# Broadcast copies loaded one chunk at a time over all 128 partitions, and the first tile's work rearranged

## The chip, the cores and the metric

The kernel runs on one core of a Trainium2 chip. The metric is the device time of one execution in microseconds. Engines are named as in the profile: PE (TensorE, with its weight loads PEld), DVE (VectorE), ACT (ScalarE), POOL (GpSimd), SP (SyncE, which here only issues DMAs). An engine name with a q (SPq) is that engine's sequencer issuing DMAs.

## The reference, cut to what matters

```
e  = stack of 32 gathered rows, one per table      # (B=1024, M=32, D=16)
x1 = relu(einsum('bmd,bhd,mhk->bkd', e, e,  W0))   # h over 32
x2 = relu(einsum('bmd,bhd,mhk->bkd', e, x1, W1))   # h over 64, K = 64
x3 = relu(einsum('bmd,bhd,mhk->bkd', e, x2, W2))
z  = concat(sum_d x1, sum_d x2, sum_d x3)          # (B, 192)
h  = concat(z, dense_ctx); two relu layers (512, 256), then one output
```

All of it is in float32.

## The kernel before, in words

The batch is cut into 8 tiles of 128 rows, and each tile into two blocks by the embedding dimension d (8 of 16 values each), so there are 16 blocks of N = 8 x 128 = 1024 columns. A block has three layers. For each layer an engine multiplies pairs of (m, h) rows elementwise into a product tile z of 128 partitions x 2 x 1024, and PE contracts it with a 128x64 weight chunk into the accumulators. Layer 0 has two such pairs and a small extra one; layers 1 and 2 have eight each (four in the order NAT, four in SWP, in which the halves of h are swapped between partitions).

The first factor of a layer-1 or layer-2 product is x1 or x2, which ACT spreads from the accumulators into the banks xq (for DVE) and xs (for POOL). The second factor is `x0b[s]` (s is the half of d): for every chunk c of 8, partition p holds row 4c + p // 32 of the transposed embeddings, so each row of 4 KB is repeated over 32 partitions. A chunk over all partitions is 512 KB, and `x0b[s]` has 8 chunks, 4 MB. Pair j uses chunks 2j and 2j + 1. SP loads it from the DRAM scratch tensor `x0t`, for every block anew, in eight DMAs of 512 KB (`load_x0b`, line 371): one for each group r of 32 partitions and each half of the chunks. The half signals `x0b_in[s][half]`. The two buffers alternate: the one of the next block is loaded while the present block computes, and the load is issued when DVE has finished layer 2 of the block before. `load_l0` (lines 376 to 382) loads what layer 0 of a coming block needs: `x0_rep` (512 KB), four `x0_rot` chunks (512 KB each), `x0_lo` and `x0_hi` (64 KB each). SP issues in program order; in each tile it also writes the next tile's transposed embeddings to `x0t` (line 389, `write_half`) and waits until they are written before the next `load_l0`.

POOL gathers the embedding rows by indirect DMA, 32 for each tile (line 447), spread over the blocks by `gathers(b)`, and makes 3 of the 16 products of a block (line 472); DVE makes the others (line 529, and lines 549 in halves for the first of each layer-2 order).

Tile 0 is different. 13 of its tables are gathered; the other 19 (1000 or 1250 rows) are loaded whole into 125 partitions (line 426), and PE picks the line by a one-hot product (`pick_lines`), DVE masks and sums the row (`mask_rows`, `pick_rows`, lines 642 and 652) into `emb0`. PE transposes the four groups of 128 columns in the order GROUPS = (2, 0, 1, 3) (`transpose_group`), ACT moves them to `emb_t` and issues the writes to `x0t` (`move_first_tile`). Meanwhile the first layer 0 doesn't wait for DRAM: DVE makes its products with batch rows on partitions (line 698, eight of 128x512, `z0`), reading `emb0` with the columns of one table 16 apart; PE transposes them (line 1044), ACT copies them to `z_dve` (line 800). DVE makes the masks (lines 677 to 683) and the symmetric weights of layer 0 (lines 685 to 690) between the picks and these products. SP issues the tables' loads, then all 16 loads of the layer-1 and layer-2 weights `w_cin` (line 430), then `x0b[0]` in 16 DMAs of 256 KB (two chunks at a time, a group as soon as it is written). ACT's queue loads the MLP weights before it does anything else, and ACT orders them (lines 929 and 931) ahead of the first x1.

Of the kernel before, what the change touches and what calls it, by code (L numbers as in the profile page):

```python
# [28 lines left out]
WARM_FIRST_X = 5  # L29
# [6 lines left out]
def cin_tower(nc, dense_t, ids, tables, w0, w1, w2, wt1, bt1, wt2, bt2, wt3, out):  # L36
# [46 lines left out]
    def l1_dve(b):  # L83
        return [(v, j) for v in l1_phases(b) for j in range(PAIRS) if not (v == NAT and j in pool_l1(b))]
# [4 lines left out]
    def l1_order(b):  # L89

        if b == 0:
            return [(NAT, 0), (NAT, 1), (NAT, 2), (NAT, 3), (SWP, 0), (SWP, 1), (SWP, 2), (SWP, 3)]
# [66 lines left out]
    with ExitStack() as ctx:  # L159
# [76 lines left out]
        emb0_wrap = emb0_flat[:, M * D:M * D + M // 2 * D]  # L236
# [4 lines left out]
        def emb0_columns(table, d, dims):  # L241

            whole = x0b[1][:, :, :]
            return bass.AP(whole.tensor, table * D + d, [list(whole.ap[0])] + dims)
# [20 lines left out]
        emb0_wrapped = sem("emb0_wrapped")  # L265
# [10 lines left out]
        mlp_ordered = sem("mlp_ordered")  # L276
        x0b_in = [[sem(f"x0b_in_{s}_{half}") for half in range(2)] for s in range(HALVES)]
# [21 lines left out]
        ze_used = sem("ze_used")  # L299
        x1_ready = [sem("x1_nat_ready"), sem("x1_swp_ready")]  # L300
# [22 lines left out]
        def x0b_ready(t, s, j):  # L323

            first = 2 * 4 * 16 if s == 0 else 4 * 16
            return x0b_in[s][j // 2], 4 * 16 * t + first
# [34 lines left out]

        block = ctx.enter_context(nc.Block())

        @block.sync
        def _(sp):
# [26 lines left out]

            def load_dense(t):
# [3 lines left out]
            def body(t):  # L397
                first_tile, last_tile = isinstance(t, int) and t == 0, isinstance(t, int) and t == TILES - 1
                for k in range(2):
                    if not is_last(t, k):  # L400
# [5 lines left out]
                        for half in range(2):  # L406
                            load_x0b(t + k, 1 - k, CH // 2 * half, CH // 2 * (half + 1))
# [19 lines left out]
            for l, (w, w_in) in enumerate(((w1, w1_in), (w2, w2_in))):  # L427
                for v in (NAT, SWP):
                    for r in range(4):
                        sp.dma_start(w_cin[l][Q * r:Q * r + Q, v, :, :],  # L430
                                     bass.AP(w.tensor, r * K * K + (r + v) % 2 * Q * K,
# [514 lines left out]
        def _(pe):  # L946
# [231 lines left out]
            for i in range(len(BATCHES) + 2):  # L1178
# [4 lines left out]
                if i == 6:  # L1183
                    transpose_group(0)
# [40 lines left out]
```

## Time and profile before

| | us |
|---|---|
| three runs | 630.64, 631.96, 633.41 (median 631.96) |
| the profiled execution | 630.55 |
| its span in the profile | 628.7 |
| granted TensorE clock, mean | 0.984 of full |
| busy: PE, DVE, POOL, ACT | 594.6, 585.8, 443.2, 355.5 |
| DMA | 119.82 MB, mean 191 GB/s |

The span runs from the first to the last instruction of the core; the time of the execution is 1.85 us longer. In the profile a share of the DMA is the mean busy share of the core's 16 DMA engines; where two packets overlap on one, it passes 1. In a stretch cut into 40 slices, a digit is that share in tenths (9 is 0.9 or more).

### The profile page before, as it was taken

Reading aid. Unit: us, or ns where it says so; the run is one execution under the profiler, and the core shown is the slowest. Engines: PE = TensorE matmul, PEld = TensorE weight load, DVE = VectorE, ACT = ScalarE, POOL = GpSimd, SP = SyncE. Lnnn points to the kernel's source line nnn. Section 1 sums busy time; section 2 is a strip of 40 time slices with the busy share of each in tenths; the row PEclk is TensorE's granted clock in tenths of the full one; section 3 lists DMA queues with packets and bytes.
Section 4 is the critical chain, followed back from the end, with each engine's and each line's share of the span. In section 5 each row is a group of like instructions: output and inputs, shape, how many; then the busy total and the mean of one; then the engine's idle time right before and its main releaser. Section 6 shows DMA issues by size and latency. Waiting matters only on the chain.

```text
span 628.7 us, 8924 instructions
## 1 busy us (share of the span) xinstructions
PE 594.6 (95%) x3046; PEld 243.0 (39%) x3046; DVE 585.8 (93%) x398; ACT 355.5 (57%) x665; POOL 443.2 (70%) x305
## 2 busy tenths in 40 slices
PE   4398998999999999999999999999999999999988
PEld 4252332234343354334443354334443354334434
DVE  4759999999999989999999999999999999999873
ACT  0173754729394663829385574829385674829361
POOL 5767887888888884988878887988878460806120
PEclk9579999999999999999999999999999999999999
DMA  6899989994997689695999779795999789690000
GB/s 176 192 236 271 210 249 210 274 211 113 252 264 183 137 248 214 205 218 128 238 218 246 154 231 213 230 217 129 221 216 258 155 247 217 212 213 17 2 0 1
DMA packets 60175, 119.82 MB, mean 191 GB/s; under 512 B 15271, under 2 KB 33734, under 8 KB 60054
## 3 DMA queue, kind: packets, MB, share of 16 engines
q1 hardware_dynamic: 49414, 114.69, 73.7%
q0 software_dynamic: 7584, 1.96, 3.8%
q10 hardware_dynamic: 3152, 2.86, 1.7%
q8 instruction: 13, 0.21, 0.2%
q14 instruction: 12, 0.10, 0.1%
HBM read 115.27 MB, written 5.25 MB: 192 GB/s over the span
## 4 chain that ended last, share of the span: by engine, by line
PE 53%; POOL 21%; DVE 12%; issue 7%; ACT 3%; SPq 2%; DMA 1%; DVEq 0%; ACTq 0%; POOLq 0%
PE acc L968 47%; POOL emb L447 12%; POOL z_pool L472 8%; DVE z_dve L529 8%; PE psm L1071 2%; SPq L426 2%; PE psm L1079 2%; DMA x_rot<-in_tbl_dram 1%; DVE z_dve L549 1%; DVE x0b L698 1%; PE acc L983 1%; ACT xq L717 1%; ACT xq L725 1%; ACT xq L771 1%; PE psm L1086 1%
## 5 line engine op out<-in xcount | busy, mean ns | idle before, releaser
L529 DVE TENSOR_TENSOR z_dve<-xq,x0b 128x2048 f32<-128x2048 f32 x179 | 398.5, 2279 | 12.4 <-ACT xq L717 7.5
L968 PE MATMUL acc<-z_dve,w_cin 128*64 128x512 f32 x1688 | 387.2, 597 | 9.9 <-DVE z_dve L529 7.1
L472 POOL TENSOR_TENSOR z_pool<-x0b,xs 128x2048 f32<-128x2048 f32 x45 | 205.3, 4565 | 89.4 <-ACT xs L717 88.9
L447 POOL DMA_INDIRECT emb<-in_tbl_dram,ids_all x224 | 218.3, 974 | 66.3 <-issue 61.3
L968 PEld LDWEIGHTS acc<-z_dve,w_cin 128*64 128x64 f32 x1688 | 127.3, 136 | 230.5 <-issue 166.9
L754 ACT ACTIVATE xq<-acc 64x512 f32<-64x512 f32 x64 | 36.5, 570 | 123.1 <-PE acc L968 122.4
L968 PE MATMUL acc<-z_pool,w_cin 128*64 128x512 f32 x360 | 85.0, 593 | 1.4 <-POOL z_pool L472 1.3
L549 DVE TENSOR_TENSOR z_dve<-xq,x0b 128x1024 f32<-128x1024 f32 x64 | 75.8, 1215 | 6.9 <-ACT xq L754 5.0
L717 ACT ACTIVATE xs<-acc 64x512 f32<-64x512 f32 x124 | 73.4, 592 | 1.7
L771 ACT ACTIVATE xq<-acc 32x512 f32<-32x512 f32 x128 | 72.2, 564 | 1.9
L725 ACT ACTIVATE xq<-acc 32x512 f32<-32x512 f32 x128 | 72.2, 564 | 1.7
L529 DVE TENSOR_TENSOR z_dve<-xq,x_rot 128x2048 f32<-128x2048 f32 x30 | 67.1, 2277 | 0.0
L968 PE MATMUL acc<-z_dve,w_sym 128*64 128x512 f32 x256 | 58.2, 594 | 1.0 <-DVE z_dve L529 1.0
L780 ACT COPY xq<-x_rep 128x512 f32<-128x512 f32 x30 | 16.6, 587 | 69.4 <-DVE z_dve L529 69.4
L968 PEld LDWEIGHTS acc<-z_pool,w_cin 128*64 128x64 f32 x360 | 25.6, 137 | 53.0 <-issue 48.4
L717 ACT ACTIVATE xq<-acc 64x512 f32<-64x512 f32 x64 | 36.5, 570 | 7.1 <-DVE z_dve L529 5.3
L968 PEld LDWEIGHTS acc<-z_dve,w_sym 128*64 128x64 f32 x256 | 18.1, 137 | 38.3 <-issue 34.2
L1019 PE MATMUL acc<-x_rot,z_dve 125*128 125x128 f32 (+1 forms) x38 | 9.9, 428 | 9.6 <-DMA x_rot<-in_tbl_dram 9.6
L983 PEld LDWEIGHTS acc<-z_extra,w_extra 128*64 128x64 f32 x256 | 15.1, 137 | 9.1 <-issue 9.1
L447 POOL DMA_INDIRECT x0b<-in_tbl_dram,ids_all x13 | 12.5, 959 | 7.1 <-issue 3.4
L983 PE MATMUL acc<-z_extra,w_extra 128*64 128x128 f32 x256 | 16.7, 273 | 0.0
L787 ACT ACTIVATE zrelu<-acc 128x512 f32<-128x512 f32 x24 | 14.3, 597 | 0.6
(99 smaller groups left out, 241.8 us busy)
## 6 DMA issues: line engine op xcount, KB each, us to landing
x0b<-x0t SPq DMA_DIRECT2D x120, 512.0 KB, 13.2
x_rot<-x0t SPq DMA_DIRECT2D x60, 512.0 KB
x_rep<-x0t SPq DMA_DIRECT2D x15, 512.0 KB, 7.9
x0b<-x0t SPq DMA_DIRECT2D x16, 256.0 KB, 8.1
emb<-in_tbl_dram,ids_all POOLq DMA_INDIRECT x224
x0t<-emb_t SPq DMA_DIRECT2D x28, 128.0 KB
w_cin<-in_L_rec_W_dram SPq DMA_DIRECT2D x16, 64.0 KB
x_lo<-x0t SPq DMA_DIRECT2D x15, 64.0 KB
```

The costliest lines, as they stand in the source:

```text
L447: nc.gpsimd.indirect_dma_start(out=rows[:, D * f:D * f + D], out_offset=None, in_=tables[f], in_offset=bass.IndirectOffsetOnAxis(ap=ids_al ...
L472: nc.gpsimd.tensor_tensor(z_pool[:, n % ZP_SLOTS, :, :], x0b[b % 2][:, 2 * j:2 * j + 2, :], xs[l - 1][:, :].unsqueeze(1).broadcast_to([P, ...
L529: nc.vector.tensor_tensor(z_dve[:, base % Z_SLOTS, :, :], in0.unsqueeze(1).broadcast_to([P, 2, N]), in1, ALU.mult).then_inc(z_made, 1)
L549: ins = nc.vector.tensor_tensor(z_dve[:, n % Z_SLOTS, :, columns], bank(k, 3 + v)[:, columns].unsqueeze(1).broadcast_to([P, 2, NH]), x0b[k ...
L717: ins = nc.scalar.activation(out_tile[K * half:K * half + K, NH * side:NH * side + NH], acc[l][K * side:K * side + K, :], ACT.Relu)
L725: ins = nc.scalar.activation(out_tile[Q * r:Q * r + Q, NH * side:NH * side + NH], acc[l][row:row + Q, :], ACT.Relu)
L754: ins = nc.scalar.activation(bank(k, 3)[K * half:K * half + K, NH * side:NH * side + NH], acc[1][K * side:K * side + K, :], ACT.Relu)
L771: ins = nc.scalar.activation(bank(k, 4)[Q * r:Q * r + Q, NH * side:NH * side + NH], acc[1][row:row + Q, :], ACT.Relu)
L780: ins = nc.scalar.copy(bank(k - 1, 2)[:, NH * side:NH * side + NH], x0_rep[:, NH * side:NH * side + NH])
L787: nc.scalar.activation(zrelu[l][:, :], acc[l][:, :], ACT.Relu).then_inc(zacc_set[l], 1)
L968: ins = nc.tensor.matmul(acc[l][K * side:K * side + K, :], weights[c], z[:, c, NH * side:NH * side + NH], start=start and c == 0, stop=sto ...
L983: ins = nc.tensor.matmul(acc[0][K * side:K * side + K, NE * e:NE * e + NE], w_extra[:, EXTRA // 2 * side + e, :], z_extra[:, :], start=Fal ...
```

## The change

Seven edits, all but the first in tile 0 only.

1. `load_x0b` issues one DMA for each chunk: 128 partitions of `x0b[s][:, c, :]` from a source pattern of 4 rows, each repeated 32 times, of 1024 elements. The number of DMAs of a block and their size stay 8 and 512 KB; in tile 0 they go from 16 of 256 KB to 8 of 512 KB, with a signal for each pair.
2. Layer 1 of block 0 takes the pairs in the order in which their groups are written (2, 0, 1, 3).
3. SP issues the layer-1 weights after the second group of `x0b[0]`, and the layer-2 weights after the first `load_l0`. ACT issues the MLP weights after the first x1, and orders them after `rep(0, 1)`.
4. DVE makes the masks before the ids arrive, and layer 0's weights after the first products.
5. `emb0` is copied a second time with d outermost (`emb0_by_d`): five copies by ACT, one by DVE. The first products read it there, with the tables next to each other.
6. x1 of block 0 signals after each half, and DVE makes the first pair in halves.
7. PE gets 8 + 4 small products that keep it busy around the transposes (`warm`), and one fewer of the large ones (`keep_warm`, 4 for 5).

```diff
-            def load_x0b(t, s, c0, c1):
-                for r in range(4):
-                    sp.dma_start(x0b[s][Q * r:Q * r + Q, c0:c1, :],
-                                 x0_rows(t, s, r + 4 * c0, [[0, Q], [4 * ROW, c1 - c0], [1, N]])
-                                 ).then_inc(x0b_in[s][c0 // (CH // 2)], 16)
+            def load_x0b(t, s, c0, c1, landed):
+                for c in range(c0, c1):
+                    sp.dma_start(x0b[s][:, c, :], x0_rows(t, s, 4 * c, [[ROW, 4], [0, Q], [1, N]])
+                                 ).then_inc(landed, 16)
...
-            for l, (w, w_in) in enumerate(((w1, w1_in), (w2, w2_in))):
-                for v in (NAT, SWP):
...
-            for g in GROUPS:
+            for i, g in enumerate(GROUPS):
                 sp.wait_ge(x0t0_written[g], 32)
-                load_x0b(0, 0, 2 * g, 2 * g + 2)
+                load_x0b(0, 0, 2 * g, 2 * g + 2, x0b_first_in[g])
+                if i == 1:
+                    load_cin_weights(0, w1, w1_in)
             sp.wait_ge(lines_picked, len(BATCHES))
             load_l0(0, 1)
+            load_cin_weights(1, w2, w2_in)
...
+            def first_pair_of_x1():
+                v, j = l1_dve(0)[0]
...
+                for side in range(2):
+                    columns = slice(NH * side, NH * side + NH)
+                    if side == 0:
+                        dve.wait_ge(x1_first_half, 1)
+                    else:
+                        dve.wait_ge(x1_ready[v], 1)
...
-            nc.vector.tensor_copy(emb0_wrap, emb0[:, 0:M // 2 * D]).then_inc(emb0_wrapped, 1)
+            nc.vector.tensor_copy(emb0_by_d_part(M // GRP * GROUPS[-1], M // GRP),
+                                  emb0_group(GROUPS[-1])).then_inc(emb0_turned, 1)
+            dve.wait_ge(emb0_turned, GRP + 2)
             for u in range(2 * CH0):
                 d = ND // 2 * (u % 2)
                 nc.vector.tensor_tensor(z0_flat[:, NH * u:NH * u + NH].rearrange("p (d m q) -> p d m q", m=M, q=4),
-                                        emb0_columns(0, d, [[1, ND // 2], [D, M], [0, 4]]),
-                                        emb0_columns(u // 2, d, [[1, ND // 2], [D, M], [CH0 * D, 4]]),
+                                        emb0_d_columns(0, d, [[BY_D, ND // 2], [1, M], [0, 4]]),
+                                        emb0_d_columns(u // 2, d, [[BY_D, ND // 2], [1, M], [CH0, 4]]),
                                         ALU.mult).then_inc(z0_made, 1)
...
             def move_first_tile():
                 for i, g in enumerate(GROUPS):
+                    if i < GRP - 1:
+                        act.wait_ge(gathered0[g], 16 * gathered_in(g))
+                        act.wait_ge(rows_picked, batches_of(g))
+                        nc.scalar.copy(emb0_by_d_part(M // GRP * g, M // GRP), emb0_group(g)).then_inc(emb0_turned, 1)
+                        if g < GRP // 2:
+                            nc.scalar.copy(emb0_by_d_part(M + M // GRP * g, M // GRP), emb0_group(g)).then_inc(emb0_turned, 1)
...
+            move_first_tile()
+            move_first_z()
+            first_x1_nat()
+            x1_swp(0, 0)
+            set_relu(0, 0, 0)
             act.dma_start(wt1_in[0], wt1[0:2 * K, :]).then_inc(mlp_in, 16)
...
-            move_first_tile()
-            move_first_z()
+            rep(0, 1)
             act.wait_ge(mlp_in, 6 * 16)
...
+            def warm(n):
+                for _i in range(n):
+                    for c in range(4):
+                        nc.tensor.matmul(turned_bank[3][:, P * c:P * c + P], ident[:, :], ident[:, :], start=True, stop=True)
```

## Rows read from the trace of the kernel before

**Rows 1.** The page: busy time; granted clock in 40 slices of the span.

```profile
PE 594.6 (95%) x3046; PEld 243.0 (39%) x3046; DVE 585.8 (93%) x398; ACT 355.5 (57%) x665; POOL 443.2 (70%) x305
...
PEclk9579999999999999999999999999999999999999
```

**Rows 2.** Stretches: span part, engines' busy time, PEclk, DMA share, GB/s.

```profile
290.00:360.00 70.00, 70.00 (x366) 28.37 (x366) 69.17 (x41) 42.98 (x82) 58.06 (x41) 1.00 0.90 210
...
304.00:316.00 12.00, 12.00 (x58) 4.02 (x56) 12.00 (x7) 1.20 (x3) 10.48 (x8) 1.00 1.05 200
316.00:328.00 12.00, 12.00 (x76) 5.73 (x74) 11.68 (x10) 10.88 (x19) 8.91 (x7) 1.00 1.04 201
329.00:333.00 4.00, 4.00 (x20) 1.26 (x18) 4.00 (x4) 3.91 (x9) 3.38 (x4) 1.00 1.03 394
```

**Rows 3.** SP's DMA issues in order, steady state (start, us).

```profile
298.81 5.01 SPq L371 DMA_DIRECT2D x0b<-x0t  x8
317.56 0.54 SPq L376 DMA_DIRECT2D x_rep<-x0t  x1
318.15 2.60 SPq L378 DMA_DIRECT2D x_rot<-x0t  x4
```

**Rows 4.** The page, DMA issues by line: count, KB each, landing.

```profile
x0b<-x0t SPq DMA_DIRECT2D x120, 512.0 KB, 13.2
x_rot<-x0t SPq DMA_DIRECT2D x60, 512.0 KB
...
x0t<-emb_t SPq DMA_DIRECT2D x28, 128.0 KB
w_cin<-in_L_rec_W_dram SPq DMA_DIRECT2D x16, 64.0 KB
```

**Rows 5.** DMA from 20.6 to 21.8 us, digits and GB/s in 40 slices.

```profile
DMA  8401298730013333434333334333433333333343
GB/s 188 154 0 17 68 206 307 171 137 0 17 34 69 86 87 87 87 87 87 87 87 87 88 88 105 88 71 87 88 88 87 87 87 87 87 87 87 87 87 86
```

**Rows 6.** Waits of SP's queue, whole span (us in total, times, longest).

```profile
SPq L376 <- DMA x0t<-emb_t: 12.0, 7, 2.3
```

**Rows 7.** SP's DMA issues in order, first tile.

```profile
1.24 15.41 SPq L426 DMA_DIRECT2D x_rot<-in_tbl_dram  x19
16.69 11.24 SPq L430 DMA_DIRECT2D w_cin<-in_L_rec_W_dram  x16
27.98 13.39 SPq L371 DMA_DIRECT2D x0b<-x0t  x16
```

**Rows 8.** DVE in order, first tile and last block.

```profile
26.54 1.83 DVE L652 TENSOR_REDUCE x0b<-z_dve 128x16 f32<-128x160 f32 x6
...
28.71 0.20 DVE L677 TENSOR_REDUCE diag_scale<-ident 128x1 f32<-128x32 f32 x1
...
29.44 0.21 DVE L685 TENSOR_TENSOR w_ex<-w_ex,w_exb 128x64 f32<-128x64 f32 x1
...
30.20 0.74 DVE L690 TENSOR_TENSOR w_extra<-w_ex,extra_mask 128x512 f32<-128x512 f32 x1
30.86 7.85 DVE L698 TENSOR_TENSOR x0b<-x0b 128x512 f32<-128x512 f32 x8
...
46.45 17.67 DVE L529 TENSOR_TENSOR z_dve<-xq,x0b 128x2048 f32<-128x2048 f32 x8 [7.54 <-ACT xq L717]
...
574.71 6.67 DVE L529 TENSOR_TENSOR z_dve<-xq,x0b 128x2048 f32<-128x2048 f32 x3
```

**Rows 9.** PE in order, first tile.

```profile
31.98 7.44 PE L1044 MATMUL xq<-ident,x0b 128*128 128x128 f32 x32 [2.98 <-DVE x0b L698]
...
39.46 3.65 PE L968 MATMUL acc<-z_dve,w_sym 128*64 128x512 f32 x16
```

**Rows 10.** ACT in order, first tile.

```profile
40.10 2.17 ACT L929 COPY wt<-z_pool 128x512 f32<-128x512 f32 x2
...
44.03 2.31 ACT L717 ACTIVATE xq<-acc 64x512 f32<-64x512 f32 x4 [0.72 <-PE acc L983]
```

More of the change, by code:

```diff
@@ L83, in l1_dve @@
     def l1_dve(b):
-        return [(v, j) for v in l1_phases(b) for j in range(PAIRS) if not (v == NAT and j in pool_l1(b))]
+        pairs = FIRST_PAIRS if b == 0 else range(PAIRS)
+        return [(v, j) for v in l1_phases(b) for j in pairs if not (v == NAT and j in pool_l1(b))]
     def l2_dve(b):
@@ L91, in l1_order @@
         if b == 0:
-            return [(NAT, 0), (NAT, 1), (NAT, 2), (NAT, 3), (SWP, 0), (SWP, 1), (SWP, 2), (SWP, 3)]
+            return [(v, j) for v in (NAT, SWP) for j in FIRST_PAIRS]
         if b == 1:
@@ L276, in cin_tower @@
         mlp_ordered = sem("mlp_ordered")
+        x0b_first_in = [sem(f"x0b_first_in_{j}") for j in range(PAIRS)]
         x0b_in = [[sem(f"x0b_in_{s}_{half}") for half in range(2)] for s in range(HALVES)]
@@ L323, in x0b_ready @@
         def x0b_ready(t, s, j):
-            first = 2 * 4 * 16 if s == 0 else 4 * 16
-            return x0b_in[s][j // 2], 4 * 16 * t + first
+            if isinstance(t, int) and t == 0 and s == 0:
+                return x0b_first_in[j], 2 * 16
+            return x0b_in[s][j // 2], 4 * 16 * t + 4 * 16 * s
         def bank(k, i):
@@ L360, in gathered_in, with batches_of @@
             return sum(f not in rows_in for f in range(M // GRP * g, M // GRP * g + M // GRP))
+        def batches_of(g):
+            return 1 + max(n for n, batch in enumerate(BATCHES) if any(f // (M // GRP) == g for f in batch))
         block = ctx.enter_context(nc.Block())
@@ L391, in write_half, with load_cin_weights @@
                                  emb_t[:, HG * h:HG * h + HG, :]).then_inc(x0t_written, 16)
+            def load_cin_weights(l, w, w_in):
+                for v in (NAT, SWP):
+                    for r in range(4):
+                        sp.dma_start(w_cin[l][Q * r:Q * r + Q, v, :, :],
+                                     bass.AP(w.tensor, r * K * K + (r + v) % 2 * Q * K,
+                                             [[K, Q], [4 * K * K, CH], [1, K]])).then_inc(w_in, 16)
             def load_dense(t):
@@ L589, in body @@
                     for i, (v, j) in enumerate(l1_dve(blk(t, k))):
-                        cin_pair(1, t, k, v, j, l1_phases(blk(t, k)).index(v))
+                        if first_tile and k == 0 and i == 0:
+                            first_pair_of_x1()
+                        else:
+                            cin_pair(1, t, k, v, j, l1_phases(blk(t, k)).index(v))
                         if k == 0 and i == 1 and first_tile is False:
@@ L734, in x1_nat, with first_x1_nat @@
                 spread_nat(bank(k, l1_phases(blk(t, k)).index(NAT)), 0, x1_ready[NAT])
+            def first_x1_nat():
+                act.wait_ge(*acc_done(0, 0, 0))
+                for side in range(2):
+                    for half in range(2):
+                        ins = nc.scalar.activation(bank(0, 0)[K * half:K * half + K, NH * side:NH * side + NH],
+                                                   acc[0][K * side:K * side + K, :], ACT.Relu)
+                    ins.then_inc(x1_first_half if side == 0 else x1_ready[NAT], 1)
             def x1_swp(t, k):
@@ L1027, in transpose_group @@
                 pe.wait_ge(gathered0[g], 16 * gathered_in(g))
-                pe.wait_ge(rows_picked, 1 + max(n for n, batch in enumerate(BATCHES)
-                                                if any(f // (M // GRP) == g for f in batch)))
+                pe.wait_ge(rows_picked, batches_of(g))
                 if i > 0:
@@ L1147, in body @@
                     claim(2, t, k)
+                    if first_tile and k == 0:
+                        pe.wait_ge(w2_in, 8 * 16)
                     for i, (v, j) in enumerate(l2_order(blk(t, k))):
```

79 lines of the change are left out of this document (41 added, 38 removed).

## The prediction

> **What bounds the kernel now.** I read the page's busy times first, then stretches of the steady part, SP's issues there, and the order of work in tile 0. PE is busy for 594.6 of 628.7 us [rows 1], and from 290 to 360 us it has no idle time at all while DVE works 69.17 of 70.00 and POOL 58.06 [rows 2]. A tile takes 70.65 us there (DVE begins the same three products of a block at 504.06 and at 574.71 [rows 8]), a block 35.3. So 15 blocks are PE's, DVE close behind. The DMA engines are the next resource, and they are the one that the first edit touches: their share is 0.90 over that stretch at 210 GB/s [rows 2]. The 4.19 MB of `x0b` for the next block are issued at 298.81 [rows 3] and flow at 200 GB/s until about 328 (two stretches of 12 us [rows 2]); after them the rest of the queue goes at 394 GB/s (329 to 333 us [rows 2]). Both have a DMA share above 1, so all 16 engines are occupied: one moves 200 / 16 = 12.5 GB/s in the first case and 394 / 16 = 24.6 in the second.
>
> **Edit 1, the chunk loads.** It adds no DMA and no byte in the steady part: eight DMAs of 512 KB (x120 for 15 blocks [rows 4]), now over 128 partitions. What can change is how many engines work on one, and how fast each goes.
>
> Rate of one engine. The loads over 32 partitions go at 12.5 GB/s an engine, the loads over 128 partitions behind them at 24.6. Taken alone this speaks for the change: 4.19 MB would take 4.19 / 0.394 = 10.6 us, not 21. (The Trainium skill, "SBUF — State Buffer", section "Door 1: The DMA port swizzle", says that 32 partitions reach only 8 of the 16 ports; the two rates agree.)
>
> Number of engines. In tile 0 the tables' loads are 125 partitions of one contiguous run each. SP has issued all 19 by 16.65 us (1.24 + 15.41 [rows 7]), and at 21 us they are still flowing: from 21.0 to 21.8 us the digits stand at 3 and the rate at 87 GB/s [rows 5]. 3 tenths is 5 of 16 engines (0.31), with a backlog waiting and eleven engines free, and 5 is the largest divisor of 125 that is not over 16. Loads whose outermost count is 32 or 128 fill all 16 [rows 2]. So a load is divided by its outermost count, and the backlog doesn't spread to other engines. The new load counts 128 on the SBUF side, but its source pattern is 4 rows, each repeated 32 times: outermost count 4. If both sides must be divided, it runs on 4 engines, and always the same 4. No row shows a load whose two sides differ in this way below 16 (`x0_rep` has 32 and 128). (The Trainium skill, "DMA: Bandwidth & Descriptors", section "Why a DMA increments its semaphore by 16 and not by 1", states it so: the slowest dimension of each side counts, the largest k up to 16 that divides both, on the lowest-numbered engines of a queue of SP; its rules add that a small outermost count confines a load to so many engines. Rows 5 agree with it for 125; that a small count on the source side alone does it, no row here shows.)
>
> I take 4 engines. At 24.6 GB/s each they move 98.5 GB/s, and a block's `x0b` takes 4.19 / 0.0985 = 42.6 us (bounds: 10.6 with 16 engines at 24.6, 84 with 4 engines at 12.5). That is above the block's 35.3 us even before the other loads, so the cover is gone and these 4 engines become the bound. Their queue never empties: `x0b` of the block after next is issued when DVE ends a block, some 31 us after the previous load has landed, and the load between takes 42.6. A load over 16 engines ends when its part on these four has ended, so all others queue there too.
>
> The sum, along the queue of those engines:
> - first `x0b` issue, as before: 28.0 [rows 7] (weights and waits move around it, a few us at most);
> - 16 loads of `x0b`: 16 x 42.6 = 682;
> - 15 `load_l0` of 5 x 0.524 + 2 x 0.066 = 2.75 MB, all over 128 partitions: 2.75 / 0.394 = 7.0 each, 105 (x60 `x0_rot` [rows 4]);
> - 28 writes to `x0t` of 0.131 MB and 16 weight loads of 0.066 MB [rows 4]: 4.7 MB / 394 = 12;
> - in each tile SP waits for a write before it issues `load_l0`; the write is queued behind `x0b` on these engines, so they run dry while it lands: 12.0 us in all, as SP's wait is now [rows 6];
> - together 839, when the last block's second half of chunks lands. DVE needs it from the third product of that block on, at 574.71 + 2 x 2.2 = 579.1 [rows 8]; from there to the end of the span it is 628.7 - 579.1 = 49.6.
>
> That gives 889 of span and, with 1.9 around it, 890 us. It is made against the profiled execution (630.55), which is 1.4 below the median; beside a change of this size that is nothing. On the low side, an engine may do 26 GB/s: 16 loads are then 645, and the sum 853. On the high side, 22 GB/s (some contention) makes 762 of them, and with PE at its lower clock in the tail (after the idle time in tile 0 it was granted 0.5 to 0.7 in slices 2 and 3 [rows 1]) about 980. PE idles some 15 us in every block, which can lower its clock elsewhere too; a block has 14 us of slack for that.
>
> **The other edits** all lie in tile 0, and behind the DMA queue they bring nothing: the second half of a block's chunks lands later than any of them matters. What they are worth if that queue is not the bound:
> - Edit 4: masks and weights stand between the picks' end (26.54 + 1.83 = 28.37) and the first product at 30.86 [rows 8]. Moved, and with a copy of about 0.3 in place of the wrap copy, the products start 2.1 earlier. The masks (28.71 to 29.44) hide in DVE's wait for the ids. The weights (29.44 to 30.86, 1.4) now come after the products, beside PE's last transposes and ACT's copies, and PE's layer 0 may wait some 0.5 for them.
> - Edit 5: the eight products take 7.85, 0.98 each; L690 makes 512 elements from contiguous rows in 0.74 [rows 8]. So 8 x 0.24 = 1.9 at most, and 0.4 if PE stays at its lower clock, where its transposes take 7.44 / 8 = 0.93 a product [rows 9]. A loss is excluded only by the rows' likeness; I take 1.2. ACT's five copies of 0.3 stand ahead of its copies to `emb_t` and delay the writes by some 0.3 each.
> - Edit 6: DVE's first product begins at 46.45, after four activations that start at 44.03 [rows 8, 10]; it can begin after two: 1.15.
> - Edit 7: 12 small products in PE's idle time cost nothing; one large one fewer is behind layer 0, in which PE waits for ACT.
> - Edits 2 and 3: SP spends 11.24 on the weights and 13.39 on `x0b` (16 issues) [rows 7]; half of the issues and the earlier start have `x0b` in place before 46 us, but DVE doesn't wait for it now. ACT's MLP copies, from 40.10 on, lie beside PE's layer 0 now and end before 44.03 [rows 10]; later ACT is idle while DVE makes products. Cover on both sides: zero.
> - Sum: 2.1 - 0.5 + 1.2 + 1.15 = 3.9 (between 2.5 and 5.5).
>
> **The rivals.**
> - *Sixteen engines: the SBUF side alone sets the count.* Then the first edit makes the loads faster than needed, the blocks stay PE's at 35.3, and only tile 0 gains: 630.55 - 3.9 = 626.6 against the profiled execution, 628.0 against the median (625 to 630). For it: `x0_rep` and `x0_rot` already have unequal counts and fill 16. Against it: 32 and 128 are both divided by 16, so they can't tell, and 125 shows that a poor divisor is obeyed. It decides if a load's digits stand at 9 while `x0b` alone flows. This is the one on the other side, faster.
> - *Four engines that meet at the same ports.* Each engine takes 32 partitions in order; if two of them keep in step they meet as the loads over 32 partitions do now, at 12.5 GB/s each. The 16 loads take 16 x 84 = 1344 in place of 682, and the time is 1552. Against it: nothing keeps two engines in step over hundreds of packets.
> - *A smaller mishap or none at all:* 16 engines, and the gain in tile 0 eaten by POOL, which is busy 58 of 70 us [rows 2] and makes one product in five: 631.
>
> **How the numbers follow.** Four engines at near full rate: 0.52, own range 850 to 1000. Sixteen engines: 0.33. Four in step, above 1000: 0.10. The rest: 0.05. The likeliest gives 890. The range must hold cases of both signs, since neither has 8 in 10: 620 to 1000, which leaves out the engines in step and the far tails. What a measurement here can tell from no change is about 0.5%, 3 us. Faster by more: 0.25 of the 0.33 and 0.01 of the rest, 0.26. Within: 0.08. Slower: 0.66.
>
> **What would show it.** Right: in a steady stretch the DMA digits stand at 2 or 3 and the rate near 98 GB/s for most of a block; DVE's first products wait for `x0b`, by some 14 us a block; `x0b` lands 40 us or more after its issue; PE's share falls to about two thirds, and tiles take near 100 us. Wrong in the count of engines: digits at 9 and near 390 GB/s while `x0b` flows, blocks of 35.3 us, DVE never waiting. Wrong in the rate: the digits at 2 or 3, but 50 GB/s. For the edits in tile 0: L698's successor starting near 28.8 and taking 0.75 a product, and the first product of layer 1 near 42.

## The result and the profile after

The changed kernel takes 922.14 us (median of 6 runs, 917.9 to 922.94). The kernel before, run beside it, takes 630.64 to 633.41 in four runs. Two more runs of it took 1038.59 and 1038.8 us in a slow state that nothing here explains, and all ratios in this text compare fast runs alone, so they are not the quotients of the medians. The ratio is 1.458, 95% interval 1.453 to 1.463. The profiled execution took 918.38 with a span of 916.5. The forecast was 890 with slower as the likeliest sign.

From the page of the changed kernel, busy time, and the rows of the clock and of the DMA in 40 slices:

```profile
PE 637.3 (70%) x3068; PEld 248.9 (27%) x3068; DVE 590.3 (64%) x399; ACT 357.0 (39%) x670; POOL 442.1 (48%) x305
...
PEclk9965979869798897959898697968989597978979
DMA  5565335633536335362356335462354424362200
```

PE works 637 of 916.5 us; before it was 594.6 of 628.7 [rows 1]. That PE's own sum rose by 43 goes with a lower granted clock: the slices show 0.5 to 0.9 of full speed where before the steady part stood at 0.9 or more. The DMA digits move between 3 and 6 where 16 busy engines would give 9. All DMA together moves 131 GB/s on average, where it was 191.

Four stretches of the changed kernel (columns as in [rows 2]). The first lies inside a load of `x0b`, the third and the fourth inside the two `load_l0` of a tile:

```profile
316.00:328.00 12.00, 12.00 (x74) 5.62 (x72) 11.69 (x7) 11.65 (x23) 9.44 (x7) 1.00 0.29 107
346.00:349.00 3.00, 0.00 (x0) 0.00 (x0) 1.46 (x1) 0.00 (x0) 0.00 (x0) 0.50 0.08 27
349.00:359.00 10.00, 9.12 (x32) 2.88 (x34) 10.00 (x6) 1.11 (x2) 0.18 (x1) 0.72 0.87 286
389.00:399.00 10.00, 0.00 (x0) 0.00 (x0) 0.00 (x0) 0.00 (x0) 5.81 (x3) 0.66 1.01 228
```

The DMA digits and rates of the changed kernel from 330 to 350 us, in 40 slices of 0.5 us, and the share of the queue that carries SP's loads from 370 to 380 us, inside another load of `x0b`:

```profile
DMA  4222222222322229222222222222222221000005
GB/s 170 102 115 98 102 106 106 106 106 98 119 106 115 98 114 288 102 106 115 98 107 106 107 107 98 106 106 115 98 98 102 103 75 57 22 9 0 0 16 164
...
q1 hardware_dynamic: 260, 1.03, 25.2%
```

While `x0b` alone flows, the digit is 2 and the rate 106 to 107 GB/s. The share of SP's queue is 25.2%, and four of sixteen is 0.25. Before, the same bytes had a share of 1.04 at 201 GB/s [rows 2]. The packets of 4096 bytes take 159 ns in the trace there (median; 315 before in the same stretch), so an engine moves 25.8 GB/s. At 26 four move 104, and 4.19 MB take 40.3 us. The zeros from 347.0 to 349.5 are the engines run dry: SP waits for a write until 348.1, and what it issues then has yet to flow.

DVE in the changed kernel, the products that waited for `x0b` (start, us, what ended the idle time):

```profile
299.79 8.88 DVE L552 TENSOR_TENSOR z_dve<-xq,x0b 128x2048 f32<-128x2048 f32 x4 [18.28 <-DMA x0b<-x0t]
...
347.54 6.69 DVE L552 TENSOR_TENSOR z_dve<-xq,x0b 128x2048 f32<-128x2048 f32 x3 [12.42 <-DMA x0b<-x0t]
...
406.50 4.49 DVE L552 TENSOR_TENSOR z_dve<-xq,x0b 128x2048 f32<-128x2048 f32 x2 [21.38 <-DMA x0b<-x0t]
```

And the sum of that wait over the span (us in total, times, longest):

```profile
DVE z_dve L552 <- DMA x0b<-x0t: 281.2, 24, 21.4
```

From 240 us on DVE waits 11.9 to 21.4 us once in every block. Before, no such wait stood in front of its steady products, and a block took 35.3 us. The products that wait for the second half of a block's chunks start at 240.43 in one block and at 874.26 in the last, twelve later: 52.8 us a block, 105.6 a tile.

SP's issues in the same stretch (start, us), one full tile:

```profile
300.40 28.07 SPq L390 DMA_DIRECT2D x0b<-x0t  x8
328.52 8.41 SPq L407 DMA_DIRECT2D x0t<-emb_t  x2
...
348.74 2.69 SPq L396 DMA_DIRECT2D x_rot<-x0t  x4
...
353.31 23.07 SPq L390 DMA_DIRECT2D x0b<-x0t  x8
376.48 11.04 SPq L394 DMA_DIRECT2D x_rep<-x0t  x1
387.56 8.38 SPq L396 DMA_DIRECT2D x_rot<-x0t  x4
```

Eight issues of `x0b` now occupy SP's queue for 28.07 and 23.07 us; before, 5.01 [rows 3]. I read this as a full queue into which SP can put nothing more, and not as a cause: with 16 engines (e1 below) eight such issues take 6.68 us. Then SP waits for the write before each second `load_l0`:

```profile
SPq L394 <- DMA x0t<-emb_t: 75.7, 7, 11.9
...
SPq L390 <- DMA x0t<-emb_t: 16.6, 2, 10.7
```

75.7 us where it was 12.0 [rows 6].

DVE in the first tile of the changed kernel, from the end of the picks:

```profile
22.27 1.84 DVE L694 TENSOR_REDUCE x0b<-z_dve 128x16 f32<-128x160 f32 x6
...
26.30 7.58 DVE L728 TENSOR_TENSOR x0b<-x0b 128x512 f32<-128x512 f32 x8 [1.36 <-ACT x0b L861]
...
41.41 2.36 DVE L588 TENSOR_TENSOR z_dve<-xq,x0b 128x1024 f32<-128x1024 f32 x2 [5.88 <-ACT xq L780]
49.87 2.29 DVE L552 TENSOR_TENSOR z_dve<-xq,x0b 128x2048 f32<-128x2048 f32 x1 [6.11 <-DMA x0b<-x0t]
67.33 2.29 DVE L552 TENSOR_TENSOR z_dve<-xq,x0b 128x2048 f32<-128x2048 f32 x1 [15.17 <-DMA x0b<-x0t]
80.23 11.08 DVE L552 TENSOR_TENSOR z_dve<-xq,x0b 128x2048 f32<-128x2048 f32 x5 [10.61 <-DMA x0b<-x0t]
```

The picks end at 24.1 (28.4 before [rows 8]), the first products run from 26.30 and the first product of layer 1 from 41.41 (46.45 before). Five microseconds are won here, and then DVE waits 6.1, 15.2 and 10.6 us for `x0b`.

### The profile page after: what moved, and what is told of

Its sections match the earlier page's. It is cut to its first block, busy times and chain, and to the rows that moved or that the text cites. A ratio compares the mean times of both kernels' runs of the same rounds, so it can differ in the third digit from the quotient of the medians.

```text
span 916.5 us, 8969 instructions
## 1 busy us (share of the span) xinstructions
PE 637.3 (70%) x3068; PEld 248.9 (27%) x3068; DVE 590.3 (64%) x399; ACT 357.0 (39%) x670; POOL 442.1 (48%) x305
## 4 chain that ended last, share of the span: by engine, by line
SPq 50%; DMA 28%; PE 13%; DVE 5%; issue 3%; ACT 1%; DVEq 0%; ACTq 0%
SPq L390 24%; DMA x0b<-x0t 19%; PE acc L1022 11%; SPq L396 8%; DMA x0t<-emb_t 7%; SPq L407 5%; DVE z_dve L552 4%; SPq L414 3%; SPq L400 2%; SPq L394 2%; SPq L398 2%; SPq L451 1%; SPq L419 1%; DMA x_rot<-x0t 1%; PE psm L1139 1%
## 5 line engine op out<-in xcount | busy, mean ns | idle before, releaser
L1022 PE MATMUL acc<-z_dve,w_cin 128*64 128x512 f32 x1688 | 426.8, 650 | 254.5 <-DVE z_dve L552 240.1
L1022 PEld LDWEIGHTS acc<-z_dve,w_cin 128*64 128x64 f32 x1688 | 132.4, 149 | 511.5 <-DVE z_dve L552 295.4
L500 POOL TENSOR_TENSOR z_extra<-x_lo,x_hi 128x128 f32<-128x128 f32 x15 | 6.9, 458 | 251.6 <-DMA x_hi<-x0t 251.6
L802 ACT ACTIVATE xq<-acc 64x512 f32<-64x512 f32 x64 | 36.5, 570 | 140.8 <-PE acc L1022 140.1
L1022 PEld LDWEIGHTS acc<-z_pool,w_cin 128*64 128x64 f32 x360 | 25.4, 137 | 57.6 <-issue 47.0
L756 ACT ACTIVATE xq<-acc 64x512 f32<-64x512 f32 x60 | 34.2, 570 | 4.7 <-ACT y_row L901 3.3
L1022 PEld LDWEIGHTS acc<-z_dve,w_sym 128*64 128x64 f32 x256 | 17.6, 137 | 40.3 <-issue 33.7
```

Of the source, the lines that this page charges most:

```text
L756: ins = nc.scalar.activation(out_tile[K * half:K * half + K, NH * side:NH * side + NH], acc[l][K * side:K * side + K, :], ACT.Relu)
L802: ins = nc.scalar.activation(bank(k, 3)[K * half:K * half + K, NH * side:NH * side + NH], acc[1][K * side:K * side + K, :], ACT.Relu)
L1022: ins = nc.tensor.matmul(acc[l][K * side:K * side + K, :], weights[c], z[:, c, NH * side:NH * side + NH], start=start and c == 0, stop=sto ...
```

## The experiments

Every experiment ran beside the kernel before on the same chip. There were three chips: one for e1 to e4 (before: 631.65), one for e5, e6, e8 and e9 (632.0), one for e10 to e13 (646.23). Where one number decides, its median over several runs is given with the ratio to before; e2, e3, e5 and e10 were run once.

**The number on the outermost place of the source pattern.** Three kernels change nothing but that pattern; sizes and DMA counts stay. None of the three computes the reference: e1 puts row p % 4 of a chunk where row p // 32 belongs, and e2 and e3 load other rows than they should. They measure the loads and nothing else.

```diff
-                    sp.dma_start(x0b[s][:, c, :], x0_rows(t, s, 4 * c, [[ROW, 4], [0, Q], [1, N]])
+ e1                 sp.dma_start(x0b[s][:, c, :], x0_rows(t, s, 4 * c, [[0, Q], [ROW, 4], [1, N]])
+ e2                 sp.dma_start(x0b[s][:, c, :], x0_rows(t, s, c // 2 * 8, [[ROW, 8], [0, 16], [1, N]])
+ e3                 sp.dma_start(x0b[s][:, c, :], x0_rows(t, s, 4 * c, [[ROW, 2], [0, 64], [1, N]])
```

> The changed kernel, but the source pattern of each chunk load has its two outer counts exchanged: 32 repeats outside, 4 rows inside. It reads the same 4 rows as often, in as many packets, but puts row p % 4 on partition p where row p // 32 belongs. Theory (the outermost count of the source sets the number of engines): 16 engines, 4.19 MB in about 10.6 us at 394 GB/s, DMA digits at 9 while x0b flows, DVE never waits for x0b, blocks of 35.3 us again; DVE's first layer-1 product stays near 41.4 where it was 46.45, so 630.6 - 5 = 625.5 us (623 to 628). Rival (the load over 128 partitions from 4 re-read rows is slow in itself, by its reads or its size): still 104 GB/s and about 920 us.

Measured: 626.07 us (4 runs), ratio 0.990 [0.986, 0.994]. Its steady part (columns as in [rows 2]):

```profile
290.00:360.00 70.00, 69.74 (x366) 28.00 (x364) 69.17 (x41) 43.14 (x80) 58.41 (x40) 1.00 0.72 210
```

The share is 0.72 where it was 0.90 for the same 210 GB/s [rows 2], and DVE is busy 69.17 of 70.00. A load over all 128 partitions on 16 engines is faster than the old one, as edit 1 meant it to be; only the count was lost. DVE in e1, the first products of layer 1 and of layer 2:

```profile
40.49 2.35 DVE L588 TENSOR_TENSOR z_dve<-xq,x0b 128x1024 f32<-128x1024 f32 x2 [5.88 <-ACT xq L780]
...
63.47 2.35 DVE L572 TENSOR_TENSOR z_dve<-xq,x0b 128x1024 f32<-128x1024 f32 x2 [0.84 <-ACT xq L802]
```

Against the kernel before (46.45 and 68.44) that is 6.0 and 5.0 us earlier, and the last block begins 4.6 us earlier (577.19 for 581.83): here the lead of tile 0 lasts to the end. The rival of sixteen engines had 626.6 for its time, and 626.07 is near it. That is in part luck, since the rival gave all of its gain (3.9) to the six other edits and none to the faster loads, and with the old loads these edits gain nothing (e4 below). No run has the loads of e1 without the six edits, so what the fast loads are worth alone is open.

> The changed kernel with a chunk load from 8 rows, each repeated 16 times (outermost count 8; the second operand holds other rows than it should). Theory: 8 engines, 8 x 25.8 = 206 GB/s, 20.3 us a block, less than the block's 35.3, so about the time of the load with 32 outside: 625 to 630 us, with DMA digits at 5 while x0b flows. Rival (slow in itself): about 920 us.

Measured: 656.02 us (1 run). Digits and the queue of SP's loads from 300 to 310 us, and two stretches:

```profile
DMA  4645464644445545455765555655556554565455
...
q1 hardware_dynamic: 524, 2.02, 50.5%
```

```profile
150.00:570.00 420.00, 416.50 (x2171) 167.99 (x2169) 412.69 (x244) 257.00 (x483) 325.57 (x213) 1.00 0.69 209
40.00:80.00 40.00, 18.71 (x60) 5.92 (x57) 13.29 (x7) 11.36 (x18) 10.26 (x12) 0.68 0.83 179
```

Half of the engines, 205 to 209 GB/s, 25.6 to 26 an engine: a block's `x0b` takes 20 us and hides in a block of 35.3. From 150 to 570 us PE is busy 416.5 of 420. The expected 625 to 630 was missed in tile 0: from 40 to 80 us DVE has 13 us of work, and of the 25.0 us that it waits for `x0b` in the whole kernel (4 times, longest 16.4) 24.6 lie there. There the load isn't hidden, whatever it is later.

> The changed kernel with a chunk load from 2 rows, each repeated 64 times (outermost count 2; the second operand holds other rows than it should). Theory: 2 engines, 51.5 GB/s, 81.4 us a block. 16 x 81.4 = 1303, and the 273 us that the changed kernel spends outside its 16 x 40.3 = 645 us of loads: about 1576 us (1500 to 1680, as the rest may shrink or grow). Rival (slow in itself): about 920 us.

Measured: 1539.31 us (1 run), granted clock 0.717. The digits from 700 to 760 us:

```profile
DMA  2111111111111111111212211111111132311111
```

Two engines at 49 to 55 GB/s while `x0b` alone flows; DVE waits 903 us for `x0b`. Counts of 2, 4 and 8 give 1/8, 1/4 and 1/2 of the engines at about 26 GB/s each. The count of 32 gives all of them, which together do less than 16 x 26: 300 GB/s at a share of 0.94 (296 to 304 us of e1). For these four counts the number of engines is the outermost count of the source side, up to 16; a count that doesn't divide 16 was not tried on that side.

(This is what the Trainium skill, "DMA: Bandwidth & Descriptors", section "Why a DMA increments its semaphore by 16 and not by 1", states. Before the change only the 125-partition loads of [rows 5] spoke for it; here the source side alone is varied and it holds.)

**Edit 1 by itself, and all but edit 1.** e5 is the kernel before with the loads (and their signals) of edit 1. e4 is the changed kernel with the old loads.

```diff
+ e5
-                for r in range(4):
-                    sp.dma_start(x0b[s][Q * r:Q * r + Q, c0:c1, :],
-                                 x0_rows(t, s, r + 4 * c0, [[0, Q], [4 * ROW, c1 - c0], [1, N]])
+                for c in range(c0, c1):
+                    sp.dma_start(x0b[s][:, c, :], x0_rows(t, s, 4 * c, [[ROW, 4], [0, Q], [1, N]])
```

> The kernel before with edit 1 alone, the chunk loads with 4 source rows outermost, in tile 0 too. Theory (the load on four engines is the whole loss): as the changed kernel, and 6 us later as its first x0b is issued at 28.0 for 21.7: 928 us (915 to 935). Rival (a part of the loss is the weights and MLP loads moved behind or between the slow loads): clearly below the changed kernel's 922, under 905 us.

Measured: 916.32 us (1 run), span 914.0, with the kernel before at 632.0 on that chip. Edit 1 is the loss. The other six edits take nothing off it; the whole change stands 2 to 7 us above e5, which one run on another chip can't tell from nothing.

> The changed kernel with only edit 1 undone: the old loads over 32 partitions, with the pair signals of tile 0. Theory: the six other edits carry their gain of tile 0 through: DVE's first layer-1 product at 41.4 for 46.45, later products not kept waiting as 4 MB of x0b at 200 GB/s from 21.7 us on are there by 43 to 45; 630.6 - 5 = 625.5 us (624 to 628). Rival (POOL or the loads behind absorb it): 630 to 632 us.

Measured: 633.24 us (10 runs), ratio 1.002 [1.000, 1.005]. The theory of 625.5 fell; with the old loads the six other edits together are worth nothing, though the first product of layer 1 starts at 41.84, 4.6 earlier than before. SP's issues tell why:

```profile
45.58 15.95 SPq L415 DMA_DIRECT2D w_cin<-in_L_rec_W_dram  x8
...
63.30 3.24 SPq L390 DMA_DIRECT2D x0b<-x0t  x6
```

The second set of weights stands between `load_l0` and the next `x0b`, its eight issues take 15.95 us behind the full queue, and the load of the next block is issued at 63.30 instead of 47.42 (43.72 in e6, which has the weights ahead again). POOL waits 5.2 us at the next `x_hi` (10.5 in all), and from 75 to 150 us DVE has 2.2 us of idle time where before it had 0.07.

**Which edit of tile 0 gains, which gives back.** e6 is e4 with both sets of weights issued ahead of `x0b[0]`, as before. e8 is e6 without the copies by d (edit 5). e9 is the kernel before with ACT's half of edit 3 alone: the MLP's loads issued after the first x1, their ordering after `rep(0, 1)`, and with it the waits of POOL and PE for the ordered weights, which the whole change moves too.

```diff
+ e6
+            load_cin_weights(0, w1, w1_in)
+            load_cin_weights(1, w2, w2_in)
...
-                if i == 1:
-                    load_cin_weights(0, w1, w1_in)
...
-            load_cin_weights(1, w2, w2_in)
```

> The changed kernel with the old loads over 32 partitions, and with both sets of layer-1 and layer-2 weights issued by SP ahead of x0b[0], as before the change (SP's half of edit 3 undone too). With the old loads alone the first layer-1 product started 4.6 us earlier (41.84) but the next block's x0b was issued at 63.3 for 47.4, behind the weights, and the gain was gone. Theory (the weights, moved into the time when the DMA queue is full, took the gain back): x0b of block 1 issued before 48, no wait of POOL for x_hi, and 631.6 - 4 = 627.5 us (625.5 to 629). Rival (the weights ahead of the tables' tail or the loads' 200 GB/s cost it anyway): 631 to 633 us.

Measured: 629.17 us (7 runs), ratio 0.996 [0.994, 0.997].

> As the kernel with the weights first, and edit 5 undone too: no second copy of the rows by d, the first products read the columns 16 apart as before. Theory (the profile of the changed kernel: products every 0.93 us for 0.97, but ACT's five copies of 0.41 hold the start back by 0.8 to 1.4 us): equal or up to 1 us faster than the kernel with the weights first. Rival (my prediction's 1.2 us for edit 5): 1.2 us slower than it.

Measured: 630.03 us (8 runs), ratio 0.996 [0.994, 0.998].

> The kernel before with ACT's half of edit 3 alone: the MLP weights loaded after the first x1 and ordered after rep(0, 1). In the changed kernel the picks ended at 24.1 us for 28.4, which I had not priced. Theory (the 0.93 MB of MLP weights lay before the small tables on the same DMA engines): picks end near 25, and 631.6 - 3 = 628.5 us (627 to 630). Rival (the layer weights' move on SP's queue did it, or nothing carries through): picks end near 28 and 631 to 633 us.

Measured: 628.61 us (12 runs), ratio 0.995 [0.994, 0.997].

DVE in e6: the first products and the first of layer 2 (its first of layer 1 is at 42.67):

```profile
27.62 7.48 DVE L728 TENSOR_TENSOR x0b<-x0b 128x512 f32<-128x512 f32 x8 [1.40 <-ACT x0b L861]
...
67.50 2.36 DVE L572 TENSOR_TENSOR z_dve<-xq,x0b 128x1024 f32<-128x1024 f32 x2 [2.08 <-PE acc L1022]
```

DVE in e8: the first products and the first of layer 1:

```profile
25.40 7.96 DVE L729 TENSOR_TENSOR x0b<-x0b 128x512 f32<-128x512 f32 x8
...
40.80 2.35 DVE L589 TENSOR_TENSOR z_dve<-xq,x0b 128x1024 f32<-128x1024 f32 x2 [5.88 <-ACT xq L781]
```

DVE in e9: the last of the picks, the first products, the first of layer 1:

```profile
22.98 1.83 DVE L653 TENSOR_REDUCE x0b<-z_dve 128x16 f32<-128x160 f32 x6
...
27.26 7.86 DVE L699 TENSOR_TENSOR x0b<-x0b 128x512 f32<-128x512 f32 x8
...
42.86 4.49 DVE L530 TENSOR_TENSOR z_dve<-xq,x0b 128x2048 f32<-128x2048 f32 x2 [7.54 <-ACT xq L718]
```

The copies by d are worth nothing. They shorten a product from 0.99 to 0.93 and not to 0.75, and they begin later: the last row copy waits for ACT, which makes five copies at 0.41 beside its moves (1.40 us of idle time ahead of them in e6). Without them the first product of layer 1 is even 1.9 earlier.

e9 gives as much as e6 and e8, which contain it. The picks end at 24.8 instead of 28.4 [rows 8], and I had priced that move at nothing. In the kernel before, ACT's queue issues the six MLP loads from 12.98 to 16.0 us (behind layer 0's weights, not before anything else), while the last tables are still on their way:

```profile
12.98 0.61 ACTq L919 DMA_DIRECT2D z_pool<-in_W_top_dram  x1
```

PE waits 9.6 us for tables there and 5.5 in e9. The layer-1 and layer-2 weights on SP's queue are not what delays the picks: these end at 25.2 with the weights behind (e4) and at 25.4 with them ahead (e6).

All three stand at 67.20 to 67.50 with the first product of layer 2, where before it was 68.44. The lead of 3.6 to 5.7 us at layer 1 is down to one there. ACT in e9:

```profile
62.77 2.18 ACT L934 COPY wt<-z_pool 128x512 f32<-128x512 f32 x2 [9.54 <-DMA bt_s<-in_b_top_dram]
...
66.14 2.35 ACT L755 ACTIVATE xq<-acc 64x512 f32<-64x512 f32 x4
```

ACT waits 9.54 us for the loads that it issued late, orders them, and only then spreads x2. In the kernel before it does that at 66.16, released by PE. In e9 PE has ended layer 1 at 62.9, so here the ordering holds x2 for about 3 us, and DVE, done with layer 0, stands idle for 2.23 us of them. In e8 it is otherwise:

```profile
65.92 2.33 ACT L803 ACTIVATE xq<-acc 64x512 f32<-64x512 f32 x4 [0.91 <-PE acc L1017]
```

ACT has ended the ordering at 65.0 and waits for PE, which before that stood idle for 4.29 us (49.5 to 53.8) until the next tile's gathered rows were there to be transposed. So in e8 it is the gathered rows, and not ACT, that hold x2. Moving the ordering away was put to the next runs.

**Moving the ordering, the gathers, and the writes.** e11 is e8, and e13 is e9, with ACT's three ordering copies behind block 0's second layer. e12 is e11 with block 0's gathers split 12, 4, 6.

```diff
-            act.wait_ge(mlp_in, 6 * 16)
-            for i in range(2):
-                nc.scalar.copy(wt1_s[i][:, :, :], ...
...
+                        if k == 0 and first_tile:
+                            act.wait_ge(mlp_in, 6 * 16)
...
- return {0: (14, 2, 6), ...
+ return {0: (12, 4, 6), ...                    # e12
```

> The loads of before, the weights issued ahead, the rows not copied by d, and ACT's three copies that order the MLP's weights moved from ahead of block 0's second layer into the body behind it, POOL asking for them in block 1 only. In e8 ACT waited 10.14 us for the MLP's loads at that place, and x2's first product ran at 67.20. Theory: that wait is where tile 0's gain is given back; x2's first product comes near 64 and the time is 626 to 627. Rival: POOL's part of block 0 holds PE there anyway, and the time stays 629 to 630.

Measured: 644.92 us (12 runs), ratio 1.000 [0.996, 1.003].

> e11 with block 0's gathers split 12, 4, 6 between the engines instead of 14, 2, 6, so that POOL has its product ready earlier (PE waited 0.6 to 1.9 us for it in the runs before). Theory: 0.5 to 1.5 us below e11. Rival: within 0.5 of it, since DVE takes over what POOL lays down.

Measured: 644.07 us (median of 12 runs), ratio 0.997 [0.993, 1.000].

> The kernel before with only the MLP's loads issued late by ACT (as e9, 628.6) and the three ordering copies moved behind block 0's second layer. Theory: ACT's wait of 9.54 us for these loads no longer holds x2, and the time is about 626.5. Rival: what holds x2's first product at 67.4 is the product chain of DVE and POOL, and the time stays at 628.6.

Measured: 645.02 us (12 runs), ratio 1.001 [0.997, 1.004].

These ran on another chip, where the kernel before took 646.23 (29 runs, 641.23 to 648.95), so only the ratios speak. e11 and e13 are level with before, so e13 lacks even e9's 0.5%, and e12's 0.3% reaches to nothing and overlaps with e11. Their traces show why the chips can't be compared step by step. Engines' busy time in e13, two stretches (columns as in [rows 2]), and DVE around them:

```profile
22.00:24.00 2.00, 0.04 (x1) 0.00 (x0) 0.00 (x0) 0.00 (x0) 1.42 (x2) 1.00 0.70 140
24.00:26.00 2.00, 0.00 (x0) 0.00 (x0) 0.00 (x0) 0.00 (x0) 1.66 (x2) 0.81 0.60 130
```

```profile
28.78 0.93 DVE L644 SCALAR_TENSOR_TENSOR z_dve<-row_no,row_of,acc 128x160 f32<-128x160 f32 x3 [7.40 <-remote]
...
53.29 8.88 DVE L531 TENSOR_TENSOR z_dve<-xq,x0b 128x2048 f32<-128x2048 f32 x4 [9.67 <-issue]
```

From 22 to 28.8 us PE and DVE do nothing, POOL stops at 26.2, and all go on at 28.8 to 29.1, released by something outside this core's records ("remote"). e11 and e12 stop in the same way near 27 us, and in e10 PE and ACT stop from 24.3 to 35.1 us, while POOL works on to 32; the traces from the other two chips haven't. The first product of layer 1 comes at 53.29 and not at 42.86. I have no trace of the kernel before from this chip and can't say that it has the pause too, though its time suggests it. With the pause the early landing of the tables is worth nothing by this reading.

What comes after the pause can still be read. From the first product of layer 1 to the first of layer 2 DVE takes 22.0 us before (46.45 to 68.44), 24.6 in e9 with its wait of 2.23 for ACT, and 22.9 in e13 (53.29 to 76.16), where ACT spreads x2 as soon as PE releases it and DVE goes on without a wait. So the ordering costs DVE some 2 us at that place. What that is worth at the end of the kernel stays open.

e10 is the changed kernel, with the writes to `x0t` issued by ACT, right behind the copy of each half.

```diff
-                            write_half(t + 1, 1)
...
+                act.wait_ge(emb_copied, 2 * (t - 1) + h + 1)
+                write_x0t(t, HG * h, HG * h + HG, x0t_written)
```

> The changed kernel, but the writes of a tile's rows to x0t are issued by ACT, right behind its own copy of each half, and not by SP between two chunk loads. SP's waits for writes (75.7 + 16.6 = 92 us in the profile after) then begin from writes that don't stand behind x0b's loads of SP's queue. Theory: part of the 79 us that the loads themselves don't explain is this wait, and the time falls to about 880 (865 to 900). Rival: the four engines hold the backlog whichever queue issues the write, since the write's rows pass through them too, and the time stays within 5 of 922.

Measured: 916.61 us (1 run), span 914.7. SP's waits for writes in e10:

```profile
SPq L394 <- DMA x0t<-emb_t: 31.9, 7, 6.1
...
SPq L390 <- DMA x0t<-emb_t: 21.3, 2, 14.1
```

They fell from 92.3 to 53.2 us. The time followed little: 916.61 is 5.5 below 922.14, nearer to the rival's range (within 5) than to the theory's 865 to 900. From the first issue of `x0b` to the third product of the last block it is 871.30 - 23.38 = 847.9 us, against 874.26 - 21.66 = 852.6, which is 4.7 less. But e10 ran on the chip with the pause. Its fourth block has this product at 251.59:

```profile
251.59 6.68 DVE L547 TENSOR_TENSOR z_dve<-xq,x0b 128x2048 f32<-128x2048 f32 x3 [17.05 <-DMA x0b<-x0t]
```

The twelve blocks from there on take 619.7 us in e10 and 633.8 in the changed kernel, 14 less or 1.2 a block; the first four, with the pause in them, take 9.4 more. So moving the writes is worth 2.3 us a tile (103.3 for 105.6), and not the 5 that 39 us less of waiting over eight tiles suggest. SP's issues in e10:

```profile
299.57 33.27 SPq L390 DMA_DIRECT2D x0b<-x0t  x8
336.57 1.19 SPq L394 DMA_DIRECT2D x_rep<-x0t  x1
```

In this tile the queue pauses once, for 3.7 us (332.84 to 336.57). A wait of SP costs only as far as the four engines run dry in it, which was 3 us a tile in the changed kernel.

## Why the prediction was right, and by how much each term was off

The mechanism is the predicted one: one DMA on 4 of 16 engines, because of the source side's outermost count; the engines' queue as the bound; every other edit behind it. e1, e2 and e3 show the count, e5 shows that nothing else takes part. The forecast of 890 is 28 below the profiled execution. That it is so near is in part luck: one term was 79 too low, three others together 51 too high. The range of 620 to 1000, made to hold both signs, says little. The sum, term by term:

- *First issue of `x0b`*: 21.66 instead of 28.0: -6.3. The weights had gone behind it and the picks ended earlier; I had said "a few us at most".
- *One engine's rate*: 26 instead of 24.6 GB/s, so 40.3 and not 42.6 a load: -37. I had the 26 as the low end. The 394 GB/s from which 24.6 came were several kinds of loads together; the packets of `x0b` alone show 159 ns.
- *All between the loads*: 852.6 - 645 = 207.6 instead of 129: +79. This is the term that was mis-sized. It is the price of `load_l0`, 2.75 MB taken at 394 GB/s, 7.0 us. In the stretches above it flows at 286 GB/s when the queue had run dry (9.6 us) and at 228 behind a backlog (12.1 us). With 3 us dry that makes 2 x 40.3 + 9.6 + 12.1 + 3 = 105.3 for a tile; 105.6 were measured. The writes of a tile (0.52 MB, an estimate of 1.3 us at 394 GB/s) are not in this sum, so it is good to a us or two. Of the 79, some 48 lie in the last twelve blocks (633.8 - 12 x 40.3 = 150 between their loads, for the forecast's 102). The other 31 lie in the first four, where the sixteen loads of weights stand in the queue too (27 us of SP's issues) and I had 12 for weights and writes over the whole kernel.
- *The tail*: 916.5 - 874.3 = 42.2 instead of 49.6: -7.4. Nothing got faster here; I had misread the trace of the kernel before. The three products at 574.71 [rows 8] end layer 2 of the block before the last. The last block's own products begin behind them:

```profile
581.83 11.08 DVE L529 TENSOR_TENSOR z_dve<-xq,x0b 128x2048 f32<-128x2048 f32 x5 [0.45 <-issue]
```

  Its third begins near 581.8 + 2 x 2.2 = 586.2, and from there to the end it is 628.7 - 586.2 = 42.5, as in the changed kernel.
- Together 889 - 6.3 - 37 + 79 - 7.4 = 917, and the span is 916.5.

The lower clock, which I had only mentioned, is seen (mean 0.853 instead of 0.984). By the sum above it costs little: PE is idle in every block, and what its slower stretches cost lies inside that idle time. In e3 it is 0.717, and the time of 1539 still lies in the range that followed from the loads (1500 to 1680).

What would show it, as the prediction listed: digits 2 and 3 (seen), near 98 GB/s (107), DVE's waits near 14 a block (12 to 21, 17.6 on average), `x0b` landed 40 us or more after its issue (47.1 for the load issued at 300.40, whose second half DVE gets at 347.54), PE's share two thirds (70%), tiles near 100 (105.6). For tile 0: products from near 28.8 at 0.75 each (from 26.30 at 0.95) and the first of layer 1 near 42 (41.41).

The six edits of tile 0 had been priced at 3.9 us if the loads were not the bound. With the old loads they gave nothing (e4), with SP's weights back in their place 2.8 (e6). The price was wrong by its parts, though it changed no sign:

- Edit 5, 1.2: nothing (e6 against e8). A product takes 0.93, not 0.75. I took 0.75 from L690, whose pattern differs: the new products still repeat elements four times or step over them, which may be why; no run separates it. The copies by ACT take 0.41, and the products wait for them.
- Edit 3, ACT's half, 0: 3.4 us (e9), the whole of what any kernel that computes the reference won. With the six MLP loads out of the way the picks end 3.6 earlier; that they had slowed the tables' landing on the shared engines is the reading that fits, argued from this one edit and from PE's shorter wait for tables (5.5 for 9.6). I had looked only at what ACT does, not at what its queue's DMAs take from the others.
- Edit 3, SP's half, 0: a loss. 15.95 us of issues stand ahead of `x0b` of the next block (e4), and the ratio to before falls from 1.002 to 0.996 when they are moved back (e6), some 4 us. The step had put both sides at zero.
- Edits 4 and 6: the products begin at 25.40 in e8 against 27.26 in e9, 1.9 for the predicted 2.1, and the first product of layer 1 at 40.80 against 42.86, 2.1 for 2.75 (2.1 - 0.5 + 1.15). Both are gone by the first product of layer 2.

The lead at layer 1 is 3.6 to 5.7 us in the traces of e6, e8 and e9, and about 1 is left at layer 2 of block 0 (67.2 to 67.5 for 68.44). In e9 and e6 DVE loses some 2 us of it to ACT's ordering, in e8 it is PE's wait for gathered rows. By the medians 2 to 3.4 us arrive at the end, more than these traces show: their executions are among the slower of their kernels (630.33 in e9, 631.14 in e6, 632.31 in e8), the one of the kernel before among its fastest, and the last block begins at 581.19 in e9 for 581.83. Where the medians' gain is kept is not shown.

No kernel that computes the reference beats e9 here by its median, 0.5% below before; e6 and e8 can't be told from it. A chunk load on 16 engines in the right order of partitions (e1's speed: a share of 0.72 for 0.90) would need the rows of every weight chunk in another order; it was not tried.

## What to carry to other kernels

Read a load's two patterns for their outermost counts before its bytes: a count of 2, 4 or 8 on the source side alone ran on so many engines here, and the queue behind it couldn't get round them. Where the count of engines changes, work out the transfer anew from the bytes, the number of engines and the rate of one in the new shape (4.19 MB / (4 x 26 GB/s) = 40 us), and compare it with the block. The old time times 16 / 4 would have given 84, since one engine also went twice as fast in the new shape. And price a moved DMA by what it takes from the engines where it lands and what it stood beside before, also when the engine that issues it has time.

## What the runs showed of the hardware beyond that

- One engine moved 26 GB/s in packets of 4096 bytes (159 ns), and alike with 2, 4 or 8 engines at work (49 to 55, 106 to 107 and 205 to 209 GB/s, with little else in the stretch).
- The stretch with `load_l0` in it went at 394 GB/s before (329 to 333 us), at 286 behind an idle queue (349 to 359), and at 228 when `x0b` loads on four engines stood ahead and behind it (389 to 399), with all 16 at a share of 1.0. Why the 4096-byte packets take 278 ns in the last (median; 159 in the second) is open.
- SP's issue of one DMA of `x0b` took 0.6 us before (5.01 for eight) and 2.9 to 4.2 us when the loads ran on four engines (23.07, 28.07 and, in e10, 33.27 for eight).
- While `x0b` flowed, the old loads had a share of 1.04 for 201 GB/s; the loads of e1, with the same 16 engines and bytes but each over all partitions, 0.94 for 300 (296 to 304 us). Over whole blocks the shares are 0.90 and 0.72 for 210 GB/s. The median packet of 4096 bytes took 159 ns in e1 instead of 315. (The Trainium skill, "SBUF — State Buffer", section "Door 1: The DMA port swizzle", gives 32 partitions half of the ports; e1 against before agrees.)
- On one chip PE, DVE and ACT stood still together for some us between 20 and 35 us of the span in e10 to e13 (PE and DVE for 7 in e13), and the kernel before was 14 us (2.2%) slower there than on the others.
